# Layer norm, gated attention and an expert mixture on one core: another order of the fold, the first step and the last tiles, and another way for the bias column

## The chip, the cores and the metric

The kernel runs on one core of one Trainium2 chip. The metric is the device time of the kernel in microseconds (us). The engines are named as the profile names them: PE is TensorE's matrix multiply (PEld its weight load), DVE is VectorE, ACT is ScalarE, POOL is GpSimd, and SP is SyncE, which here only issues DMAs.

## The reference

The input x has 4 sequences of 1024 tokens with 512 features. Cut to what matters:

```python
xn = layernorm(x)
# attention on xn, with a layer norm of its own (gamma, beta)
x_norm = layernorm(xn) * gamma + beta
q, k, v = x_norm @ qkv[:, :512], x_norm @ qkv[:, 512:1024], x_norm @ qkv[:, 1024:]
attn = softmax(causal(q @ k.T / sqrt(512)))
s = (attn @ v) @ o_proj + xn
# experts on xn: 8 experts, the best 2 of each token, and a shared one
gates = top2_normalised(softmax(xn @ router_w.T))
routed = sum_e gates[:, e] * (silu(xn @ wg[e]) * (xn @ wu[e])) @ wd[e]     # inner width 352
shared = (silu(xn @ sg) * (xn @ su)) @ sd                                  # inner width 704
out = xn_input + s * silu(routed + shared)        # xn_input is x
```

## The kernel before

Matrices are multiplied in float16 pairs: each float32 operand is split into a high part (ACT writes it, `..._hi`, `high`) and a low part (DVE writes it, `..._lo`, `low`), and a product is three products of parts. PE's program is one long row of such products, in five stages.

**Fold** (`fold_programs`). The attention weights are multiplied together once: q with k, and v with o_proj. PE turns q and k by 128x128 transposes (eight groups, `("turn", m, n)`, each in a PSUM bank of its own), ACT and DVE split each bank. v is split, and SP turns it by four DMA transposes (L401) into `v_turned`. Then come eight products, `("product", m, n)` with m = 0 for q with k and m = 1 for v with o; `bank_of` names the bank of each. Beta gives a bias: DVE multiplies the bank of each turned q with a row of beta and sums it (`beta_row`, L602, four of them, after which the bank is free), PE multiplies small things (`beta_products`, `bias_folds`), and DVE writes `bias_q` and `bias_v` (`keep_bias`). `rows_before` says how many `beta_row` a product waits for. The load of beta and the load of o_proj count on one semaphore, `rest_loaded`. Between all this DVE also takes the statistics of the first two token tiles (`stats`, `normalise`), and splits the weights of the shared expert (`split_hi` on ACT and `split_lo` on DVE, eight pieces; pieces 0 to 3 are for gate and up, 4 to 7 for down).

**Shared expert** (`expert_stages`, the loops over `range(NT)`, 32 steps of one token tile, two units each). Unit n of PE is `unit_in` (24 matmuls, L677), and after it `unit_down` of unit n - 2 (9 matmuls, L684). A unit's chain is: PE, `silu` on ACT, `hidden` on DVE, `h_high` on ACT, `h_low` on DVE, `turn_h` on SP (a DMA transpose, L1079), and the landed transpose lets `unit_down` go. Beside it a step normalises a later tile, splits expert weights (`in_high`/`in_low` in chunks, `down_high`/`down_low`) and turns the tile (`turn_x`). All queues are served in program order, so a step that waits holds what stands behind it. Steps from `ROUTING` = 24 on also hold the routing tables, which DVE writes (`one_hot`) and PE multiplies (`hot_product`, L1283). At the end of step `LATE` + 1 = 27, ACT issues `store_bias` (L427): `bias_v`, 128 partitions of 4 floats, goes to the DRAM row `bias_row`, so that 512 single floats are written 512 bytes apart within a partition.

**Routed experts** (71 slot tiles in a hardware loop), then **attention** (`stage4`): for each sequence 16 projection groups, and 8 tiles of queries, in order `ORDER`, for the last sequence `LAST_ORDER` = 1, 3, 5, 0, 7, 4, 2, 6. A query tile t is: `scores` on PE (L1806), `soften` on DVE (mask, row maximum, L1942 to L1946), `probs` and `p_high` on ACT, `p_low` on DVE, two DMA transposes, `weigh` on PE (L1819, three matmuls for each block of 128 keys, bank `pv_banks[t % 2]`), `combine_first` and `combine` on DVE (L1967, L1975, L1979), `finish` on POOL (adds x, L1744), and the store. `end` on DVE makes the gate. PE weighs two tiles behind the scores, and `weigh(t)` waits for `combine(t - 2)`, which frees the bank.

## Time and profile before

| | us |
|---|---|
| median of three runs | 1174.65 |
| lowest, highest | 1174.34, 1176.52 |
| profiled execution, own time | 1174.52 |
| its span in the trace | 1172.8 |
| PE busy | 1140.6 |

The span runs from the first instruction of the trace to the last; 1.7 us of the profiled execution's own time lie outside it. Start times below are us from the start of the span. "Idle before" is how long the engine stood still, and the releaser is what ended that.

### The profile page before, as it was taken

How to read it: one execution, taken by the hardware profiler on the slowest of the kernel's cores; microseconds unless marked ns; L12 is line 12 of the kernel's file. 1: busy time of each engine (PE TensorE's matmuls, PEld its weight loads, DVE VectorE, ACT ScalarE, POOL GpSimd, SP SyncE). 2: the span in 40 equal slices, each digit the busy share in tenths (PEclk: the TensorE clock that was granted, in tenths of full speed). 3: DMA queues.
4: the chain of work that ended last, by engine and by line, in shares of the span. 5: the costliest groups of instructions: out<-in, count | busy, mean ns of one | idle time of the engine just before them, and what ended most of it. 6: DMA issues, size and time to landing. Idle time of an engine off the chain costs nothing. (4 is left out here: it accounts for less than half of the span.)

```text
span 1172.8 us, 21142 instructions
## 1 busy us (share of the span) xinstructions
PE 1140.6 (97%) x6608; PEld 628.7 (54%) x6609; DVE 568.8 (49%) x1168; ACT 470.2 (40%) x824; POOL 423.4 (36%) x659
## 2 busy tenths in 40 slices
PE   7999999999998999999999999999999999999996
PEld 4555555555555555555555555554444444444442
DVE  5876766676557422211211221221377467467466
ACT  4543444344422222322322322333655545645652
POOL 2253333332100122222222222211764764754754
PEclk9999999999999999999999999999999999999999
DMA  8879999989545588999899778776667767676373
GB/s 247 235 190 238 228 243 214 226 204 234 154 84 70 106 160 201 203 206 191 207 209 193 172 179 185 178 172 173 138 162 194 151 161 183 169 166 178 106 161 102
DMA packets 369410, 210.22 MB, mean 179 GB/s; under 512 B 308912, under 2 KB 319160, under 8 KB 369344
## 3 DMA queue, kind: packets, MB, share of 16 engines
q1 hardware_dynamic: 357984, 173.67, 64.5%
q0 software_dynamic: 10800, 35.69, 12.0%
q8 instruction: 36, 0.59, 0.2%
q14 instruction: 30, 0.25, 0.1%
q10 hardware_dynamic: 560, 0.02, 0.0%
HBM read 89.31 MB, written 46.01 MB: 115 GB/s over the span
## 5 line engine op out<-in xcount | busy, mean ns | idle before, releaser
L677 PE MATMUL pair<-arena 128*128 (+2 forms) x3240 | 506.4, 313 | 2.5 <-DVE arena L1466 1.5
L677 PEld LDWEIGHTS pair<-arena 128*128 128x128 f16 x3240 | 316.2, 98 | 185.6 <-issue 4.5
L684 PE MATMUL bank<-arena 128*128 (+1 forms) x1215 | 285.3, 380 | 9.6 <-DMA arena<-arena 9.6
L684 PEld LDWEIGHTS bank<-arena 128*128 128x128 f16 x1215 | 118.4, 98 | 137.9 <-DMA arena<-arena 8.2
L1531 DVE SCALAR_TENSOR_TENSOR arena<-pair,slot_unit,arena 128x352 f32<-128x352 f32 x71 | 41.4, 583 | 270.7 <-ACT arena L1447 229.5
L1447 ACT ACTIVATE arena<-pair,slot_unit 128x352 f32<-128x352 f32 x71 | 39.3, 553 | 207.1 <-PE pair L677 176.8
L1207 POOL COPY arena<-token_of 128x1 uint32 (+1 forms) x71 | 13.2, 186 | 278.8 <-DMA arena<-arena 98.4
L1819 PE MATMUL bank<-arena 128*128 128x512 f16 x432 | 98.3, 379 | 1.8 <-DVE arena L1975 1.8
L1806 PE MATMUL pair<-arena 128*128 128x512 f16 (+3 forms) x576 | 97.5, 326 | 0.6 <-ACT arena L1863 0.6
L1209 POOL DMA_INDIRECT arena<-xn_rows,arena x71 | 70.8, 998 | 55.6 <-POOL arena L1207 55.6
L1791 PE MATMUL bank<-arena 128*128 128x512 f16 x384 | 86.0, 379 | 1.6 <-PEq L1026 1.6
L1791 PE MATMUL pair<-arena 128*128 128x512 f16 x384 | 84.7, 379 | 0.0
L1806 PEld LDWEIGHTS pair<-arena 128*128 128x128 f16 x576 | 52.9, 98 | 45.8 <-ACT arena L1863 1.1
L1726 POOL DMA_INDIRECT arena<-slot_rows,arena x64 | 68.5, 1070 | 24.5 <-POOL arena L1723 21.5
L1364 ACT ACTIVATE arena<-pair,unit 128x352 f32<-128x352 f32 x64 | 35.1, 549 | 96.3 <-PE pair L677 96.0
L235 POOL TENSOR_TENSOR root_seed<-variances,minus_half 128x2 f32<-128x2 f32 x32 | 24.6, 770 | 129.8 <-DVE variances L245 129.8
L1819 PEld LDWEIGHTS bank<-arena 128*128 128x128 f16 x432 | 41.8, 98 | 50.5 <-issue 2.7
L1733 POOL TENSOR_TENSOR arena<-arena 128x512 f32<-128x512 f32 x32 | 42.4, 1325 | 65.2 <-ACT arena L1878 64.2
L1791 PEld LDWEIGHTS bank<-arena 128*128 128x128 f16 x384 | 37.5, 98 | 46.3 <-issue 2.0
L1791 PEld LDWEIGHTS pair<-arena 128*128 128x128 f16 x384 | 37.6, 98 | 45.3
L1744 POOL TENSOR_TENSOR arena<-arena 128x512 f32<-128x512 f32 x32 | 43.3, 1359 | 48.6 <-DVE arena L1979 48.4
L1466 DVE SCALAR_TENSOR_TENSOR arena<-pair,unit,arena 128x352 f32<-128x352 f32 x64 | 36.9, 577 | 47.6 <-ACT arena L1364 47.6
(186 smaller groups left out, 1178.5 us busy)
## 6 DMA issues: line engine op xcount, KB each, us to landing
slot_rows<-arena SPq DMA_DIRECT2D x71, 256.0 KB
arena<-in_L_attn_x_dram SPq DMA_DIRECT2D x64, 256.0 KB, 3.5
xn_rows<-arena SPq DMA_DIRECT2D x32, 260.0 KB, 2.6
shared_rows<-arena SPq DMA_DIRECT2D x32, 256.0 KB
arena<-shared_rows SPq DMA_DIRECT2D x32, 256.0 KB
out_dram<-arena SPq DMA_DIRECT2D x32, 256.0 KB, 2.2
arena<-in_L_ffn_wg_dram SPq DMA_DIRECT2D x32, 176.0 KB, 3.0
arena<-in_L_ffn_wu_dram SPq DMA_DIRECT2D x32, 176.0 KB, 3.3
```

What stands on the lines that cost most here:

```text
L677: last = pe.matmul(bank[:, 0:width], xt[:, a, c, :], weights(c, b, col, width), start=(c == 0 and i == 0), stop=(c == KC - 1 and i == 2))
L684: last = pe.matmul(bank[:, :], ht[:, a, c, :], weights(c, b), start=(start and c == 0 and i == 0), stop=(stop and c == HC - 1 and i == 2))
L1209: pool.indirect_dma_start(xg[u].bitcast(U32), None, xn_rows.bitcast(U32), bass.IndirectOffsetOnAxis(ap=index[u], axis=0)).then_inc(gathere ...
L1447: nc.scalar.activation(sbuf[u], g_banks[u][:, 0:H], ACT.Silu, scale=slot_unit[u][:, 0:1]).then_inc(slot_silu_done, 1)
L1466: v.scalar_tensor_tensor(sbuf[b], u_banks[b][:, 0:H], unit[:, t, 1:2], sbuf[b], ALU.mult, ALU.mult).then_inc(h_ready, 1)
L1531: v.scalar_tensor_tensor(sbuf[u], u_banks[u][:, 0:H], slot_unit[u][:, 1:2], sbuf[u], ALU.mult, ALU.mult).then_inc(slot_h_ready, 1)
L1726: pool.indirect_dma_start(c[f"y{n}", u], None, slot_rows, bass.IndirectOffsetOnAxis(ap=c[f"i{n}", u], axis=0)).then_inc(y_loaded[n][u], 16)
L1733: pool.tensor_tensor(c["y0", u], c["y0", u], c["y1", u], ALU.add).then_inc(y_summed, 1)
L1744: pool.tensor_tensor(c["res", u], c["s", t % S_AHEAD], c["x", t % X_AHEAD], ALU.add).then_inc(res_ready, 1)
L1791: last = pe.matmul(bank[:, :], left, right, start=(k == 0 and n == 0), stop=(k == KC - 1 and n == 2))
L1806: last = pe.matmul(wide[t % 2][:, col:col + w], qt[:, a, k, i * P:(i + 1) * P], x2t[b % 2][col // HALF][:, r, k, 0:w], start=(k == 0 and m ...
L1819: last = pe.matmul(pv_banks[t % 2][:, :], c["pt", t % 3][:, a * (i + 1) + k, :], vs[:, k, r, :], start=(k == 0 and n == 0), stop=(k == i a ...
```

## The change

1. **Fold.** Beta and o_proj get a semaphore each. The products (0,1) and (0,2) go to banks 6 and 7, (0,3) to bank 0, (1,0) to bank 1, and wait for none, none, one and two `beta_row`; the last three wait for the low parts of the first three instead. `beta_products` runs before the products of v and o. ACT and DVE run the same splits in another order.
2. **First step of the shared expert.** ACT and DVE get a written-out order, `first_step`: `h_high` and `h_low` of unit 0 stand ahead of the first chunk of expert weights, the down pieces 4 and 5 behind unit 1's `silu` and `hidden`, and `down_high`/`down_low` at the end.
3. **Bias.** PE turns `bias_v` (128x4) into 4x128 behind the first `unit_down` (`turn_bias`), ACT copies it at step 2 (`keep_bias_row`), and SP stores four rows of 512 bytes at step 4 (`store_bias`). The store on ACT at step 27 is gone.
4. **Last tiles.** DVE's `soften` of the last tile stands ahead of `combine` of the fourth tile before it; `end` of the last tile stands behind.
5. **Last product.** `weigh_last` computes columns 0 to 255 first (`pv_banks[1]`), then 256 to 511 (`proj_banks[0]`), 21 matmuls each of 256 columns in place of 21 of 512; `combine_last` does both halves on DVE, the addition of x with it, and SP stores each half. POOL's `finish` of the last tile is gone.

```diff
-            bank_of = list(range(2 * KC)) + [4, 0, 1, 2, 6, 7, 4, 3]
-            rows_before = (0, 1, 2, 3, 0, 0, 0, 4)
+            bank_of = list(range(2 * KC)) + [4, 6, 7, 0, 1, 4, 6, 7]
+            rows_before = (0, 0, 0, 1, 2, 0, 0, 0)
...
-                sp.dma_start(beta_rows, beta.partition_broadcast(P)).then_inc(rest_loaded, 16)
-                sp.dma_start(w_o, o_proj.rearrange("(c p) n -> p c n", p=P)).then_inc(rest_loaded, 16)
+                sp.dma_start(beta_rows, beta.partition_broadcast(P)).then_inc(beta_loaded, 16)
+                sp.dma_start(w_o, o_proj.rearrange("(c p) n -> p c n", p=P)).then_inc(o_loaded, 16)
...
-            def store_bias(act):
-                act.wait_ge(bias_made, 2)
-                act.dma_start(bias_row.rearrange("(c p) -> p c", p=P), bias_v[:, :],
-                              allow_slow_non_contiguous=True).then_inc(bias_stored, 16)
+            def store_bias(sp):
+                bias_row_kept(sp)
+                sp.dma_start(bias_row.rearrange("(c p) -> c p", p=P), affine_rows[0:KC, :]).then_inc(bias_stored, 16)
...
+            def turn_bias(pe):
+
+                pe.wait_ge(bias_made, 2)
+                pe.transpose(small[0:KC, 0:P], bias_v[:, :], ident).then_inc(group_done, 1)
+
+            def keep_bias_row(act):
+
+                act.wait_ge(group_done, len(on_pe) + 1)
+                nc.scalar.copy(affine_rows[0:KC, :], small[0:KC, 0:P]).then_inc(hi_done, 1)
...
+                    def first_step():
+
+                        silu(0, 0)
+                        h_high(0, 0)
+                        for i in in_chunks(0):
+                            in_high(i)
+                        silu(1, 1)
+                        split_hi(act, IN_SPLITS)
+                        split_hi(act, IN_SPLITS + 1)
+                        for t in normal_in(0):
+                            x_high(t)
+                        h_high(1, 1)
...
+                    def first_step():
+
+                        for t in normal_in(0):
+                            stats(dve, t)
+                        hidden(0, 0)
+                        keep_logits(0)
+                        h_low(0, 0)
+                        for i in in_chunks(0):
+                            in_low(i)
+                        for t in normal_in(0):
+                            normalise(dve, t)
+                        hidden(1, 1)
+                        split_lo(dve, IN_SPLITS)
+                        split_lo(dve, IN_SPLITS + 1)
+                        h_low(1, 1)
...
+                        for cols, bank in zip(halves, last_banks):
+                            for k in range(i + 1):
+                                for n, (a, r) in enumerate(PARTS):
+                                    last = pe.matmul(bank[:, cols], c["pt", t % 3][:, a * (i + 1) + k, :],
+                                                     vs[:, k, r, cols], start=(k == 0 and n == 0), stop=(k == i and n == 2))
+                            last.then_inc(pv_done, 1)
...
+                        for n, cols in enumerate(halves):
+                            dve.wait_ge(pv_done, t + n + 1)
+                            v.scalar_tensor_tensor(row[:, cols], last_banks[n][:, cols], c["inv", u][:, 0:1], row[:, cols],
+                                                   ALU.mult, ALU.add).then_inc(s_made, 1)
+                            dve.wait_ge(s_made, t + n + 1)
+                            v.scalar_tensor_tensor(row[:, cols], row[:, cols], 0.5 / S_Q, g[:, t % QT, cols], ALU.mult, ALU.mult
+                                                   ).then_inc(o_made, 1)
+                            dve.wait_ge(o_made, t + n + 1)
+                            v.tensor_tensor(res[:, cols], row[:, cols], x_row[:, cols], ALU.add).then_inc(last_added, 1)
...
+                            if t == NT - 1:
+                                combine(t - 4)
                             if n > 2:
                                 combine_first(t - 3)
                             if n > 0:
                                 p_low(t)
-                            if n > 2:
+                            if n > 2 and t != NT - 2:
                                 combine(t - 3)
```

The order on DVE in the fold, before. L595 is `low` (bank 4 to 7: turned k; `arena<-arena`: v or o), L602 a `beta_row`, L241 begins `stats`, L253 to L261 are `normalise`:

```order
5 L595 SCALAR_TENSOR_TENSOR arena<-bank6,arena 128x512
6 L595 SCALAR_TENSOR_TENSOR arena<-bank7,arena 128x512
7 L602 ISA arena<-pair0,arena 128x512
...
9 L241 BN_STATS moments<-arena 128x6
...
13 L602 ISA arena<-pair0,arena 128x512
...
15 L595 SCALAR_TENSOR_TENSOR arena<-arena 128x512 x4
```

The same place now, where `low` is L611 and `beta_row` L618:

```order
L611 SCALAR_TENSOR_TENSOR arena<-pair,arena 128x512 x4
L241 BN_STATS moments<-arena 128x6
...
L611 SCALAR_TENSOR_TENSOR arena<-bank,arena 128x512 x4
L611 SCALAR_TENSOR_TENSOR arena<-arena 128x512 x4
...
L261 TENSOR_SCALAR arena<-arena,mean_var,kept 128x512
L611 SCALAR_TENSOR_TENSOR arena<-bank,arena 128x512
...
L618 ISA arena<-pair,arena 128x512
```

The four low parts of v, behind which SP turns v, moved ahead of every `beta_row`, and the statistics of tile 0 moved between the two halves of the turns.

ACT in the first step of the shared expert, before. L1364 is `silu`, L1376 `in_high`, L1370 `h_high`, L221 `split_hi`, L265 the high part of a token tile:

```order
23 L1364 ACTIVATE arena<-pair,unit 128x352
24 L1376 ACTIVATE arena<-arena 128x704
25 L1370 CAST arena<-arena 128x352
26 L221 ACTIVATE arena<-arena 128x2x512
27 L221 ACTIVATE arena<-arena 96x512
28 L265 CAST arena<-arena 128x512
29 L1380 ACTIVATE arena<-arena 128x512
30 L1364 ACTIVATE arena<-pair,unit 128x352
```

The same place now, where `silu` is L1389, `h_high` L1395 and `in_high` L1401:

```order
26 L1389 ACTIVATE arena<-pair,unit 128x352
27 L1395 CAST arena<-arena 128x352
28 L1401 ACTIVATE arena<-arena 128x704
29 L1389 ACTIVATE arena<-pair,unit 128x352
30 L221 ACTIVATE arena<-arena 128x2x512
31 L221 ACTIVATE arena<-arena 96x512
32 L265 CAST arena<-arena 128x512
33 L1395 CAST arena<-arena 128x352
```

Unit 0's `h_high` moved ahead of the chunk of expert weights, and unit 1's `silu` ahead of the down pieces and of tile 2.

DVE at the last tiles, before. L1951 is `p_low`, L1942 begins `soften`, L1975 and L1979 are `combine`, L1965 and L1967 `combine_first`:

```order
930 L1951 TENSOR_TENSOR arena<-arena 128x384
931 L1975 SCALAR_TENSOR_TENSOR arena<-bank,arena 128x512
932 L1979 SCALAR_TENSOR_TENSOR arena<-arena 128x512
933 L1942 TENSOR_TENSOR pair<-pair,arena 128x128
...
938 L1951 TENSOR_TENSOR arena<-arena 128x896
```

The same place now, where these lines are L2022, L2013, L2046 and L2050, L2036 and L2038:

```order
934 L2022 TENSOR_TENSOR arena<-arena 128x384
935 L2013 TENSOR_TENSOR pair<-pair,arena 128x128
...
938 L2046 SCALAR_TENSOR_TENSOR arena<-bank,arena 128x512
939 L2050 SCALAR_TENSOR_TENSOR arena<-arena 128x512
...
942 L2022 TENSOR_TENSOR arena<-arena 128x896
```

The last tile's `soften` moved ahead of one `combine`.

## Rows read from the trace of the kernel before

**Rows 1.** The page: each engine's busy time, share of the span and instructions

```profile
PE 1140.6 (97%) x6608; PEld 628.7 (54%) x6609; DVE 568.8 (49%) x1168; ACT 470.2 (40%) x824; POOL 423.4 (36%) x659
```

**Rows 2.** PE's waits: releaser, then us in total, times, longest

```profile
PE bank L684 <- DMA arena<-arena: 9.6, 8, 3.0
```

**Rows 3.** PE's timeline, fold and first steps: start, duration, line, count [idle before]

```profile
17.49 8.03 PE L486 MATMUL pair<-arena 128*128 128x512 f16 x36 [1.44 <-DVE arena L602]
26.37 2.76 PE L486 MATMUL bank<-arena 128*128 128x512 f16 x12 [0.85 <-DMA arena<-arena]
...
39.14 10.98 PE L677 MATMUL pair<-arena 128*128 128x360 f16 x72
51.30 2.10 PE L684 MATMUL bank<-arena 128*128 128x512 f16 x9 [1.17 <-DMA arena<-arena]
54.87 3.74 PE L677 MATMUL pair<-arena 128*128 128x352 f16 x24 [1.47 <-DVE arena L1466]
59.59 2.10 PE L684 MATMUL bank<-arena 128*128 128x512 f16 x9 [0.97 <-DMA arena<-arena]
```

**Rows 4.** DVE's timeline of the same stretch

```profile
12.14 2.48 DVE L595 SCALAR_TENSOR_TENSOR arena<-bank,arena 128x512 f16<-128x512 f32 x4 [1.65 <-ACT arena L553]
16.74 0.69 DVE L602 CUSTOM_DVE_ANT_0 arena<-pair,arena 128x512 f32<-128x512 f32 x1 [2.12 <-DMA arena<-in_L_attn_o_proj_dram]
...
19.18 2.49 DVE L595 SCALAR_TENSOR_TENSOR arena<-arena 128x512 f16<-128x512 f32 x4
...
33.03 1.61 DVE L226 SCALAR_TENSOR_TENSOR arena<-arena 128x1408 f16<-128x1408 f32 x1
...
47.88 0.52 DVE L1471 TENSOR_TENSOR arena<-arena 128x352 f16<-128x352 f32 x1
```

**Rows 5.** ACT's timeline: the first chunk of expert weights

```profile
46.25 0.79 ACT L1376 ACTIVATE arena<-arena 128x704 f16<-128x704 f32 x1 [2.73 <-DMA arena<-in_L_ffn_wu_dram]
```

**Rows 6.** The `turn_h` issued at 356.2, alone, and the time to its landing

```profile
L1079 SPq DMA_TRANSPOSE arena<-arena x1: 1211/1211/1211, 356.2 to 356.2; - x1
...
DMA to landing us min/median/max: 12.9/12.9/12.9
```

**Rows 7.** The store of the bias on ACT, and the time to its landing

```profile
L427 ACTq DMA_DIRECT2D bias_row<-bias_v x1: 417/417/417, 355.8 to 355.8; - x1
...
DMA to landing us min/median/max: 10.0/10.0/10.0
```

**Rows 8.** PE's timeline behind it

```profile
369.16 3.24 PE L684 MATMUL bank<-arena 128*128 128x512 f16 x9 [2.99 <-DMA arena<-arena]
372.20 0.69 PE L1283 MATMUL bank<-arena 128*128 128x71 f16 x8
372.69 4.09 PE L677 MATMUL pair<-arena 128*128 128x352 f16 x24
```

**Rows 9.** A stretch: length, busy us of engines, granted clock (PEclk), DMA share, GB/s

```profile
371.00:373.00 2.00, 2.00 (x14) 1.03 (x13) 2.00 (x6) 0.56 (x1) 0.00 (x0) 0.50 0.01 2
```

**Rows 10.** PE's timeline near the end

```profile
1111.80 1.47 PE L1806 MATMUL pair<-arena 128*128 128x256 f16 x12
...
1147.03 10.67 PE L1819 MATMUL bank<-arena 128*128 128x512 f16 x48
1159.52 4.69 PE L1819 MATMUL bank<-arena 128*128 128x512 f16 x21 [1.82 <-DVE arena L1975]
```

**Rows 11.** DVE's timeline at the end

```profile
1149.96 0.29 DVE L1942 TENSOR_TENSOR pair<-pair,arena 128x128 f32<-128x128 f32 x1
...
1156.84 1.68 DVE L1967 TENSOR_TENSOR arena<-arena 128x512 f32<-128x512 f32 x1
...
1164.36 0.75 DVE L1975 SCALAR_TENSOR_TENSOR arena<-bank,arena 128x512 f32<-128x512 f32 x1 [1.18 <-PE bank L1819]
1165.21 0.69 DVE L1979 SCALAR_TENSOR_TENSOR arena<-arena 128x512 f32<-128x512 f32 x1
```

**Rows 12.** POOL's timeline at the end

```profile
1165.98 1.26 POOL L1744 TENSOR_TENSOR arena<-arena 128x512 f32<-128x512 f32 x1 [1.69 <-DVE arena L1979]
```

160 lines of the change are left out of this document (97 added, 63 removed).

## The prediction

> **What bounds the kernel now.** I read the page first: PE is busy 1140.6 of 1172.8 us [rows 1], and no other engine passes half the span. So the kernel is as long as PE's program plus PE's stops, and a change that leaves the products alone can only win back stops, or the tail behind PE's last matmul. The waits of PE come next: the largest sum is unit_down waiting for its DMA transpose, 9.6 us in 8 waits [rows 2]. PE's timeline then says where the stops are. They lie in three places. In the fold and the first steps: 1.44, 0.85, 1.17, 1.47 and 0.97 us [rows 3]. At 369 us one of 2.99 us, behind which 9 matmuls take 3.24 us where they otherwise take 2.10 [rows 8, 3]. At the end 1.82 us ahead of the last product [rows 10], and then the tail: PE's last matmul ends at 1159.52 + 4.69 = 1164.2, POOL's addition at 1165.98 + 1.26 = 1167.2 [rows 10, 12], and the store takes what is left of the span, 5.6 us. Between these places PE hardly stops, so what is won in one of them should reach the end. I add the gains up against the profiled execution's own 1174.52 us, which is within 0.02% of the median, 1174.65.
>
> **Part 1, the fold.** The 1.44 us stop goes. PE's second product had to wait for a beta_row, and DVE began that at 16.74, when o_proj had landed [rows 4]. Now the second and third product need no beta_row, and run from 17.49 - 1.44 = 16.05 us on. Three products took 8.03 us [rows 3], 2.68 each, so the fourth starts at 21.4 and needs one beta_row. DVE's turns of k end at 12.14 + 2.48 = 14.6, the low parts of v take 2.49 more and end at 17.1 [rows 4], then come one normalise, one low part, three small operations and the beta_row, an estimate of 3.3 us: 20.4. That is 1.0 us early. The 0.85 us stop goes as well: SP turned v behind low parts that began at 19.18 [rows 4] and now begin at 14.6, so the first halves land near 26.37 - 4.6 = 21.8, and the first product of v and o comes at 16.05 + 3 x 2.68 + 0.8 for beta_products = 24.9. What is late next is the split of o_proj, which now stands behind three more operations on DVE; by the same counting it ends near 25.1, and its last quarter is needed at 26.8. So the fold ends 2.3 us earlier, and unit 0 starts at 39.14 - 2.29 = 36.85.
>
> **Part 2, the first step.** A unit takes 3.7 us (three in 10.98 [rows 3]). Units 0, 1 and 2 then end at 40.6, 44.4 and 48.1. DVE is nearly full in the fold: from 25.1 on it has four split pieces of 1.61 us [rows 4] and some 10.5 us of other work, and ACT keeps it waiting some 1.5 us, so hidden of unit 0 comes at 43.6. With h_high straight behind it, h_low ends at 45.1, not at 47.88 + 0.52 = 48.4 [rows 4]. The transpose took 51.30 - 48.4 = 2.9 us [rows 3], so it lands at 48.0, when PE arrives. But unit_down also wants down pieces 4 and 5, and here I expect the new stop. Their low parts stand on DVE behind the first chunk's low part, normalise of tile 2 and hidden of unit 1, and the chunk waits for its load, which landed at 46.25 [rows 5]. I let it land 1.9 us earlier, as the normalise of tile 1 ahead of it on SP does. Then 44.4 + 5.5 us of work (0.8 on ACT, 0.9, 1.4, 0.6 and 1.8 on DVE) is 49.9, and unit_down starts at 50.0 against 51.30. Behind it the 1.47 us stop is gone (hidden of unit 1 is long done), unit 3 ends at 55.7, and the next transpose, behind tile 2's on SP, lands near 56.2 against 59.59. So PE is 3.4 us ahead there. The one added transpose on PE costs at most a small matmul's 0.2 us, and sits on the path: **3.2 us** for parts 1 and 2. The ends: 0.8 us if DVE falls another 2.4 us behind, 4.9 us if all five stops of rows 3 go, less one small one. The few later stops of 0.8 to 1.3 us up to 110 us I leave as they are, since the chains of the tiles move as PE does.
>
> **Part 3, the bias.** The turn_h issued at 356.2 took 12.9 us to land [rows 6], against 2.9 us at the start. In between lies the bias store, issued 0.4 us before it and landed after 10.0 us [rows 7]: at 365.8, and the transpose at 369.1, just where PE goes on. It moves 2 KB, but as 512 single floats. Without that hold the transpose lands at 359.1, seven us before PE needs it. The stop of 2.99 us goes, and so does what the slow clock cost behind it: 3.24 - 2.10 = 1.14, some 0.25 of the 0.69, and 4.09 - 3.74 = 0.35 [rows 8, 3]. The granted clock falls from 1.00 to 0.50 there, 2.4 to 1.2 GHz, after PE had stood 3 us [rows 9]. The sum is 4.7 us. DVE writes one_hot tables there almost without a pause, and only won part of that time, so PE meets it sooner at the hot products; I give back 0.5: **4.2 us**, ends 3.0 and 4.7. In its place PE gets the one transpose (counted), ACT one copy of 4x128 at step 2, with slack on ACT, and SP one store of four rows at step 4, 0.4 us of issue on a queue that waits for its tiles there anyway.
>
> Here a rule speaks against me. What the rows show is one transpose of 12.9 us beside one store of 10.0 [rows 6, 7]. The Trainium skill ("DMA: Bandwidth & Descriptors", section "Queues, rings and completion order") says that each DMA engine takes turns between the queues a packet at a time, so another queue's transfer should delay a transpose by its turns, not by its whole length. By the rule the hold has another cause and stays, and the sum has 0 here in place of 4.2.
>
> **Part 4, the last tiles.** The last soften began at 1149.96, behind a combine of 1.4 us [rows 11]; now it is first, and its softmax and transposes come 1.4 us earlier. The 1.82 us stop before the last product was for combine of the tile two before it [rows 10], which in turn stood behind end and a combine_first held to 1.68 us by POOL [rows 11]. PE is through with that tile's product after 39 of the 48 matmuls, at 1147.03 + 39 x 0.222 = 1155.7 [rows 10], and DVE can now take it at once: done at 1156.6, before PE wants to go on at 1157.7. So that stop goes too.
>
> **Part 5, the last product.** 12 matmuls of 256 columns took 1.47 us [rows 10], 0.11 each when the tail of the last is taken off, so 42 take 4.7 us, as 21 of 512 did. PE ends near 1162.5, not 1164.2. But then DVE is late. It has end, combine_first and combine of the tile before, and combine_first of the last: with two holds by POOL's finishes of up to 1.1 us each, combine of the tile before ends near 1161.5, and its next addition at 1162.2. Then six half operations of 0.4 to 0.5 us (0.75 and 0.69 for whole ones [rows 11]), the second of which waits for POOL until about 1163.4: the last ends near 1165.4, against 1167.2 for POOL before [rows 12]. The 5.6 us behind stay. **1.9 us** for parts 4 and 5; 3.3 us if POOL never holds DVE, and 0.8 if the last transposes are late or each hold is doubled.
>
> **The sum.** 3.2 + 4.2 + 1.9 = 9.3 us, and 1174.5 - 9.3 = **1165.2 us**.
>
> **The rivals.** (A) The hold at 356 us is not the store's, or ends elsewhere: parts 1, 2, 4 and 5 alone, 5.1 us, **1169.4**. Against it speaks that the store and the transpose begin and end within 0.4 and 3.3 us of each other. (B) The fold gives nothing: DVE is the full engine there, each beta_row and split only changed places, and PE stops at unit 1 or at the first unit_down for pieces that come as late as before. Then 4.2 + 1.9 = 6.1 us, **1168.4**. For it speaks that my DVE schedule has margins of about 1 us over some 25 operations. (C) Both: 1.9 us, **1172.6**. (D) The slower one: the store of the bias holds the transposes whatever its form, and has only moved from step 27 to step 4. There the transposes have no spare time (7 us at 359): a hold of 12.9 - 2.9 = 10 us falls on PE whole, with 1.7 us of slow clock behind. Then 3.2 + 4.2 + 1.9 - 11.7 = -2.4, **1176.9**. It decides from a hold of some 7.6 us on. Against it: four rows of 512 bytes are 4 pieces, not 512. (E) It does not do what it says: the last product in halves ends no earlier, since DVE has twice the operations. That is inside the low end of part 5.
>
> **How the numbers follow.** The forecast of 1165.2 with its bounds has 0.64, (A) 0.12, (B) 0.13, (C) 0.05, (D) 0.05, and 0.01 is for the rest. The bounds of the parts give gains from 0.8 + 3.0 + 0.8 = 4.6 to 4.9 + 4.7 + 3.3 = 12.9 us, 1161.6 to 1169.9. Both ends at once are unlikely at the fast side, so the range is 1162.0 to 1170.5, which takes in (A) and (B) and leaves out (C) and (D). A measurement of this kernel can tell about 0.2%, 2.3 us, from no change: faster 0.89 (forecast, A, B), same 0.06 (C and the rest), slower 0.05 (D).
>
> **What would show it.** Part 1: no stop ahead of the second product, and unit 0 starting at 36.9. Part 2: h_low of unit 0 before 45.5, a first unit_down near 50 released by DVE's split, not by the DMA. Part 3: no stop near 360, all turn_h landing in 3 to 5 us there, the clock 1.00 throughout, and the store of four rows landing in some 2 or 3 us with no longer stops around step 4. Parts 4 and 5: the last product following the one before without a pause, and DVE's last addition near 1158.0 in its own trace (1165.4 less the 7.4 us won before). The prediction is wrong if a transpose behind the new store takes over 8 us, or if PE stops for over 3 us in the first step, where the clock would fall as well.

## The result, and the profile after

The changed kernel takes 1162.55 us (median of four runs, 1161.58 to 1162.77), against 1175.59 for the kernel before in the same session. The ratio is 0.9885, with a 95% interval of 0.9866 to 0.9904: faster by 1.15%, 13.0 us. The forecast was 1165.2 with a range of 1162.0 to 1170.5. The profiled span went from 1172.8 to 1160.6 us, 12.2 us less. That is what the rows below have to explain.

The page (compare [rows 1]): TensorE's busy time is the same to 0.2 us, so in sum the gain is stops and tail.

```profile
span 1160.6 us, 21195 instructions
PE 1140.8 (98%) x6630; PEld 630.9 (54%) x6631; DVE 564.5 (49%) x1172; ACT 471.0 (41%) x825; POOL 425.4 (37%) x658
```

PE's waits (compare [rows 2]: 9.6 us in 8 waits on the same transposes):

```profile
PE bank L702 <- DMA arena<-arena: 4.7, 2, 3.4
PE bank L1890 <- DMA arena<-arena: 1.2, 1, 1.2
```

PE's timeline of fold and first steps (compare [rows 3]; L695 is `unit_in`, L702 `unit_down`, L541 the turned bias). The last row is a later place without a stop before it, which had 113.73 before:

```profile
16.42 5.35 PE L486 MATMUL bank<-arena 128*128 128x512 f16 x24
...
36.97 10.98 PE L695 MATMUL pair<-arena 128*128 128x360 f16 x72
47.82 2.10 PE L702 MATMUL bank<-arena 128*128 128x512 f16 x9
49.76 0.27 PE L541 MATMUL bank<-arena,bias_v 128*4 128x128 f32 x1
49.87 3.74 PE L695 MATMUL pair<-arena 128*128 128x352 f16 x24
57.01 4.00 PE L702 MATMUL bank<-arena 128*128 128x512 f16 x9 [3.40 <-DMA arena<-arena]
...
110.08 2.11 PE L702 MATMUL bank<-arena 128*128 128x512 f16 x9
```

The way to read such a pair of traces is the **lead**: the start of one and the same piece of work before, less its start after. It is 39.14 - 36.97 = 2.17 us at unit 0, 3.48 at the first `unit_down` (51.30 against 47.82), 5.00 at unit 3 (54.87 against 49.87), and only 2.58 at the next `unit_down` (59.59 against 57.01), since there stands a stop of 3.40 us that nobody had before. Behind it 9 matmuls take 4.00 us in place of 2.10, and a stretch of the table by windows has the granted clock at 0.50, that is 1.2 in place of 2.4 GHz:

```profile
58.00:60.00 2.00, 2.00 (x7) 0.63 (x5) 1.59 (x3) 1.88 (x4) 1.94 (x2) 0.50 1.11 268
```

At 65 us the lead is gone. At 110 us it is back, 3.65 us (113.73 against 110.08): the stops of 1.3, 0.9 and 0.8 us that the kernel before still has up to there are missing now. At 344 us it is still 3.65. These are the leads of one pair of executions; how far they differ in others is told ahead of the experiments. Then comes the place of the bias store. The `turn_h` transposes from 340 to 400 us land in 2.7 to 4.5 us (compare [rows 6]) and PE has no stop for them (compare [rows 8]):

```profile
L1098 SPq DMA_TRANSPOSE arena<-arena x10: 1211/1216/1581, 341.5 to 394.9; - x10
...
DMA to landing us min/median/max: 2.7/2.7/4.5
```

Behind it the lead is 8.07, so the bias gave 4.42 us. Between 400 and 1110 us it grows to 8.85. Most of that is the slot tiles of the routed experts: there PE stands for DMA transposes of such tiles for 1.01 us in two places before and for 0.31 in one now. The rest, 12.2 - 8.85 = 3.35 us, is won at the end. PE's, DVE's and POOL's timelines there (compare [rows 10 to 12]):

```profile
1138.18 10.52 PE L1878 MATMUL bank<-arena 128*128 128x512 f16 x48
1149.90 4.76 PE L1890 MATMUL bank<-arena 128*128 128x256 f16 x42 [1.20 <-DMA arena<-arena]
```

```profile
1155.73 0.48 DVE L2063 SCALAR_TENSOR_TENSOR arena<-bank,arena 128x256 f32<-128x256 f32 x1 [1.80 <-DMA out_dram<-arena]
...
1158.02 0.43 DVE L2069 TENSOR_TENSOR arena<-arena 128x256 f32<-128x256 f32 x1
```

```profile
1153.35 1.71 POOL L1803 TENSOR_TENSOR arena<-arena 128x512 f32<-128x512 f32 x1 [2.28 <-DVE arena L2050]
```

The last addition ended at 1167.24 before (POOL) and ends at 1158.45 now (DVE): a lead of 8.79, no more than at 1138 us. By the last addition, then, parts 4 and 5 gave nothing. But behind it the span went on for 5.56 us before and goes on for 2.15 us now. What stands there is seen only in the instructions that end the block: on each queue a DRAIN, and behind it the semaphore by which the engines meet. Before, and after (count, duration in ns, start):

```profile
L1644 POOLq DRAIN  x1: 6611/6611/6611, 1165.9 to 1165.9; - x1
L1644 SPq DRAIN  x1: 7/7/7, 1169.5 to 1169.5; - x1
L1644 ACTq EVENT_SEMAPHORE  x1: 17/17/17, 1172.7 to 1172.7; - x1
```

```profile
L1700 POOLq DRAIN  x1: 7057/7057/7057, 1153.3 to 1153.3; - x1
L1700 SPq DRAIN  x1: 7/7/7, 1160.4 to 1160.4; - x1
L1700 ACTq EVENT_SEMAPHORE  x1: 17/17/17, 1160.6 to 1160.6; - x1
```

SP comes to its DRAIN once the stores have landed. Before that was at 1169.5, and everybody then waited 3 us more for POOL, whose DRAIN ended at 1172.5, 5.3 us behind the end of POOL's last addition. After, POOL's last addition (tile 30's) ends at 1155.06 and its DRAIN at 1160.4, again 5.3 us later, in the same tenth as the landing of the last store.

### The profile page after: what moved, and what is told of

The parts are those of the page before. It is cut to its first block and busy times, and to the rows that moved or that the text cites. A ratio compares the mean times of both kernels' runs of the same rounds, so it can differ in the third digit from the quotient of the medians.

```text
span 1160.6 us, 21195 instructions
## 1 busy us (share of the span) xinstructions
PE 1140.8 (98%) x6630; PEld 630.9 (54%) x6631; DVE 564.5 (49%) x1172; ACT 471.0 (41%) x825; POOL 425.4 (37%) x658
## 5 line engine op out<-in xcount | busy, mean ns | idle before, releaser
L695 PE MATMUL pair<-arena 128*128 (+2 forms) x3240 | 507.1, 313 | 0.3 <-DMA arena<-arena 0.3
L695 PEld LDWEIGHTS pair<-arena 128*128 128x128 f16 x3240 | 316.6, 98 | 183.7 <-issue 1.8
L702 PE MATMUL bank<-arena 128*128 (+1 forms) x1215 | 286.0, 381 | 4.7 <-DMA arena<-arena 4.7
L702 PEld LDWEIGHTS bank<-arena 128*128 128x128 f16 x1215 | 119.1, 98 | 132.1 <-issue 7.7
L1878 PE MATMUL bank<-arena 128*128 128x512 f16 x411 | 93.4, 379 | 0.0
L1850 PE MATMUL bank<-arena 128*128 128x512 f16 x384 | 86.0, 379 | 1.6 <-PEq L1045 1.6
L1389 ACT ACTIVATE arena<-pair,unit 128x352 f32<-128x352 f32 x64 | 35.3, 552 | 111.4 <-PE pair L695 110.6
```

The lines of the kernel that those rows point to most:

```text
L695: last = pe.matmul(bank[:, 0:width], xt[:, a, c, :], weights(c, b, col, width), start=(c == 0 and i == 0), stop=(c == KC - 1 and i == 2))
L702: last = pe.matmul(bank[:, :], ht[:, a, c, :], weights(c, b), start=(start and c == 0 and i == 0), stop=(stop and c == HC - 1 and i == 2))
L1850: last = pe.matmul(bank[:, :], left, right, start=(k == 0 and n == 0), stop=(k == KC - 1 and n == 2))
L1878: last = pe.matmul(pv_banks[t % 2][:, :], c["pt", t % 3][:, a * (i + 1) + k, :], vs[:, k, r, :], start=(k == 0 and n == 0), stop=(k == i a ...
```

## The experiments

Times below are of profiled spans unless they are called medians. Most of the kernels were run once, and one and the same code does not stand at the same time in every execution. The kernels of five of the runs below are the changed kernel up to 110 us (one of them but for the place of one small store). These are PE's times in them:

| trace | first product of the fold | unit 0 | the place at 110 us | from unit 0 to there |
|---|---|---|---|---|
| before | 12.89 | 39.14 | 113.73 | 74.59 |
| changed | 11.65 | 36.97 | 110.08 | 73.11 |
| four rows on ACT | 13.00 | 36.65 | 108.22 | 71.57 |
| last addition on POOL | 13.77 | 37.41 | 108.95 | 71.54 |
| in place | 12.13 | 35.77 | 110.23 | 74.46 |
| POOL done early | 14.43 | 38.07 | 110.97 | 72.90 |
| part 4 undone | 12.85 | 36.49 | 109.91 | 73.42 |

The first column differs with the loads of the first 10 us, the last one mostly with the slow clock. So the lead at 110 us, 3.65 us in the pair above, is anything from 2.8 to 5.5 us, and a difference of spans under some 3 us shows nothing by itself. I compare distances within a run where I can.

### The bias store

**Part 3 alone**, put into the kernel before (with PE's turn and ACT's copy of it):

```diff
-            def store_bias(act):
...
+            def store_bias(sp):
+                bias_row_kept(sp)
+                sp.dma_start(bias_row.rearrange("(c p) -> c p", p=P), affine_rows[0:KC, :]).then_inc(bias_stored, 16)
...
```

> The kernel before with part 3 of the change alone: the bias column is turned by PE, copied by ACT at step 2, and stored as four rows by SP at step 4. If the 512 single floats of the store made the hold of the transposes at 356 us, all turn_h there land in under 5 us, the stop of 2.99 us and the slow clock behind it go, and the span is 4.4 us shorter than 1172.8, near 1168.4 (4.42 us is what PE's program won there in the changed kernel). If the hold comes from something else at that place, the span stays within 1 us of 1172.8. If a store of the bias holds transposes whatever its form, a stop of some 10 us comes near 97 us and the span is over 1178.

Median 1170.52 (six runs) against 1174.77, ratio 0.9967 [0.9952, 0.9982]; the span is 1168.1, 4.7 us less. The `turn_h` of 340 to 400 us land in 2.7 to 4.3 us, PE has no stop for them, and the one of 1.82 us at the end stays as it was. Across the old place of the store the lead goes from -0.40 us (362.54 against 362.14) to 4.04 (387.05 against 391.09). So part 3 is worth 4.44 us by itself, as in the sum (4.42).

**Form, queue or place?** The change altered all three. So, in the changed kernel: the four rows, but on ACT at step 27, where the single floats had been (this store reads memory that is used for other things by then, so the bias in it is not the reference's).

```diff
-                        if s == 4:
-                            store_bias(sp)
...
+                        if s == LATE + 1:
+                            store_bias(act)
```

> The changed kernel with the store of the four rows back on ACT at the end of step 27, so that the queue and the place are those of before and only the form is new. If the form made the hold: no stop near 352 us, span within 0.7 us of the changed kernel's 1160.6. If the queue or the place made it: a turn_h of over 10 us and a stop of some 3 us there, span near 1165.

The `turn_h` there land in 2.7 to 3.9 us. The span is 1158.8, 1.8 us under the changed kernel's where at most 0.7 was expected; that lead, 1.86 us, is all there at 110 us already, most of it because the clock did not fall at 57 us in this execution. At the old place PE stops only for DVE's tables:

```profile
356.63 0.45 PE L1304 MATMUL bank<-arena 128*128 128x71 f16 x8 [0.55 <-DVE arena L955]
```

And the reverse, the 512 single floats on SP at step 4:

```diff
-                sp.dma_start(bias_row.rearrange("(c p) -> c p", p=P), affine_rows[0:KC, :]).then_inc(bias_stored, 16)
+                sp.dma_start(bias_row.rearrange("(c p) -> p c", p=P), bias_v[:, :],
+                             allow_slow_non_contiguous=True).then_inc(bias_stored, 16)
```

> The changed kernel, but the store at step 4 on SP takes the 512 single floats from bias_v, as the store before did; queue and place are the new ones. If the form holds the transposes wherever it stands, the next transposes on SP take some 10 us longer, PE stops for 7 to 10 us near 97 us with a slow clock behind it, and the span is 8 to 12 us over 1160.6. If the hold needs a second queue (the store on ACT's, the transposes on SP's), the span stays within 1 us.

The span is 1170.0, 9.4 us more, and 8.9 of them are there at the first table products (367.38 against 358.49). The transpose of a token tile issued behind the store took 12.1 us to land (first fence), the hidden pieces' one 12.4, and PE stood 6.09 us for it (second fence):

```profile
L284 SPq DMA_TRANSPOSE arena<-arena x1: 1244/1244/1244, 95.9 to 95.9; - x1
...
DMA to landing us min/median/max: 12.1/12.1/12.1
```

```profile
110.84 4.02 PE L703 MATMUL bank<-arena 128*128 128x512 f16 x9 [6.09 <-DMA arena<-arena]
```

The hold belongs to the form. With single floats it is there from ACT at step 27 and from SP at step 4 (12.9, 12.1, 12.4 us). With four rows it is in neither place: behind the changed kernel's store at 93.3 the transposes up to 125 us land in 2.7 to 4.0 us. That settles rivals A and D. Nor does it hold transposes alone: in this last run the plain store of a token tile issued at 97.2 took 11.9 us and the load of x at 97.8 took 11.5, where the load at 89.7, ahead of the floats, took 3.4.

### The first step

**Part 2 undone**, the new order of the fold kept:

```diff
-                        if s == 0:
-                            first_step()
-                            continue
...
+                        if s == 0:
+                            split_hi(act, IN_SPLITS)
+                            split_hi(act, IN_SPLITS + 1)
```

> The changed kernel with part 2 undone: ACT and DVE do the first step of the shared expert in the order of before, the fold as changed. If the fold's order alone brings what parts 1 and 2 bring together (3.65 us at 110 us), unit_down of unit 115 stands where it did in the changed kernel. By my sum the fold gives 2.2 us at unit 0 and the first step's order the rest: then stops of 1 to 1.5 us come back ahead of the first unit_down and of unit 3, and PE is at 110 us some 2 us ahead of the kernel before, span near 1162.

The span is 1164.3. The gain of the fold is there at first (`unit_down` at 48.68 against 51.30) and is then handed back in the old order's own stops:

```profile
52.27 3.74 PE L695 MATMUL pair<-arena 128*128 128x352 f16 x24 [1.38 <-DVE arena L1491]
56.88 2.10 PE L702 MATMUL bank<-arena 128*128 128x512 f16 x9 [0.88 <-DMA arena<-arena]
81.05 2.12 PE L702 MATMUL bank<-arena 128*128 128x512 f16 x9 [1.57 <-DMA arena<-arena]
100.80 3.73 PE L702 MATMUL bank<-arena 128*128 128x512 f16 x9 [2.62 <-DMA arena<-arena]
```

The `unit_down` that has 110.08 after and 113.73 before is at 113.58 here: a lead of 0.15. About 2 us had been expected. So in this execution the fold's lead of 2.27 us at unit 0 (36.87) is handed back by 110 us; 1.63 us of that is the slow clock behind the stop of 2.62 us (3.73 us for 9 matmuls), which another execution need not have. From unit 0 to the 110 us place it takes 76.71 us, against 71.5 to 74.5 in the six traces with the written-out first step: that is worth 2.2 to 5.2 us. What it moved is the chain of token tiles. POOL's memset behind the low piece of tile 3 starts at 64.65 before, at 62.05 here and at 58.24 after; counted from the start of unit 0 that is 25.5, 25.2 and 21.3 us.

**The 3.40 us stop.** SP's timeline around it in the changed kernel (L284 turns tile 2, L290 stores it, L1050 is a load, L1098 is `turn_h(1)`):

```profile
50.54 1.24 SPq L284 DMA_TRANSPOSE arena<-arena  x1
51.82 0.58 SPq L290 DMA_DIRECT2D xn_rows<-arena  x1
52.45 0.44 SPq L1050 DMA_DIRECT2D arena<-in_L_attn_x_dram  x1
52.93 1.22 SPq L1098 DMA_TRANSPOSE arena<-arena  x1
```

DVE had the hidden pieces ready at 47.64 + 0.51 = 48.15, but SP stood before the tile until 50.54. I put `turn_h(1)` ahead of the tile:

```diff
+                        if s == 1:
+                            turn_h(1)
                         for t in routed_in(s)[:1]:
                             pass_x(t)
...
-                        if s > 0:
+                        if s > 1:
                             turn_h(2 * s - 1)
```

> The changed kernel, but at step 1 SP issues the transpose of unit 1's h ahead of the transpose, store and load of tile 2. h_low of unit 1 is ready at 48.2 and its transpose is issued at 52.9 in the changed kernel, behind tile 2's. My theory: that order on SP makes the stop of 3.40 us at 57; here it lands by 52 and the stop is gone, with the slow clock. But PE then runs into what the chain of the token tiles allows: that chain is 6.4 us earlier than in the kernel before (the last x_low ahead of POOL's memset ends at 58.2 against 64.6), PE at 110 us only 3.65, so some 2.7 us are to be had, the rest comes back as stops between 60 and 115 us. Span near 1158. Rival: nothing limits it behind, and the whole 3.4 us and the clock's 3 us are won: 1154. Other rival: the transpose of tile 2 comes later and PE stops for it instead: 1160.

The stop is gone, and the clock stays there. But the span is 1162.3. Other stops of the same kind came in its place, and behind the longest the clock fell after all (granted clock 0.50 from 101 to 103 us):

```profile
61.78 2.12 PE L702 MATMUL bank<-arena 128*128 128x512 f16 x9 [0.26 <-DMA arena<-arena]
79.44 2.12 PE L702 MATMUL bank<-arena 128*128 128x512 f16 x9 [0.88 <-DMA arena<-arena]
98.86 3.22 PE L702 MATMUL bank<-arena 128*128 128x512 f16 x9 [2.30 <-DMA arena<-arena]
```

At the 110 us place PE is at 111.63. This run had begun late, with unit 0 at 39.31; from there it took 72.32 us, which is inside the 71.5 to 74.5 of the same code without the edit. So no gain can be told from this run, and the later span is no loss either.

**The chain of the tiles.** One long link of it is a memset of 6.92 us on POOL, in front of tile 4's seed. I moved it to step 12, alone and then with the edit above:

```diff
                     x_low(pool, 3)
-                    if HR < P:
-                        pool.wait_ge(shared_lo, len(splits))
-                        pool.memset(w_down[HR:P, :, HC - 1], 0.0).then_inc(down_padded, 1)
-                        pool.wait_ge(down_padded, 1)
...
                     for s in range(2, LATE):
+                        if HR < P and s == 12:
+                            pool.wait_ge(shared_lo, len(splits))
+                            pool.memset(w_down[HR:P, :, HC - 1], 0.0).then_inc(down_padded, 1)
+                            pool.wait_ge(down_padded, 1)
```

> The changed kernel with one edit: GpSimd's memset of the down weights' padding rows (6.92 us at 58.24 in the changed kernel's trace, between the low piece of tile 3 and the seed of tile 4) goes from there to step 12 of the unit loop. If the stops that came back when the hidden pieces' transpose was put ahead (0.26, 0.88 and 2.30 us at 61.8, 79.4 and 98.9) are those of the chain of the next token tiles, this memset is one of its links: the seed of tile 4 comes up to 6.9 us earlier. Alone, with the 3.4 us stop still there (it belongs to a transpose queued behind another on the sync queue), TensorE should gain nothing: the unit_down after the stop at 57.0, the one at 110 us within 0.3 us of 110.08, span 1160.3 to 1160.9. Rival: the tiles' chain held in the changed kernel too, hidden in short stops: then 0.5 us or more less at 110 us. A second rival: the memset costs at step 12 what it cost at step 1, and a stop appears near 130 us: longer by up to 3 us.

Alone it gives nothing: PE is 1.29 us later than in the changed kernel right behind the long stop (58.30 against 57.01, the loads came later here), and 1.10 later at 110 us (111.18 against 110.08). From unit 0 that is 74.47 us, the slow end of the spread. The span is 1161.8.

> Both edits together: the transpose of the hidden pieces of unit 1 ahead of that of token tile 2 on the sync queue, and GpSimd's 6.92 us memset moved to step 12. With the first edit alone the stops behind 57 us came back as 0.26, 0.88 and 2.30 us, and unit_down stood at 111.63 at a place where the changed kernel has 110.08. If the memset is the link that makes them, they go, and so does the 3.4 us stop with the slow clock behind it (1.9 us): the unit_down at 110 us at 105.0 to 107.0 and the span 3 to 5 us below 1160.6, 1155.6 to 1157.6. Rival: the chain of the tiles has another pace (each tile's transpose waits for its turn among the hidden pieces' transposes on the same queue): the 0.9 and 2.3 us stops stay, and the span is 1160 to 1162.5.

Together they do: the 2.30 us stop shrank to 0.86 and 0.29, the clock did not fall there, and PE is at 106.97 at the 110 us place, as expected, and 3.1 us ahead at the table products (355.38 against 358.49). From unit 0 to the 110 us place it takes 68.75 us, 2.8 less than the shortest of the six. The span is 1159.0, not the 1155.6 to 1157.6 expected, for PE then stood for the transpose of a slot tile. It was issued at 599.4 and took 9.1 us to land, where those at 588.3 and 614.0 took 3.8 and 3.5; what held it no run shows:

```profile
608.68 3.75 PE L695 MATMUL pair<-arena 128*128 x24 [1.90 <-DMA arena<-arena]
```

### The last tiles

**Part 4 undone**, the last softmax back behind the combination:

```diff
-                            if t == NT - 1:
-                                combine(t - 4)
...
-                            if n > 2 and t != NT - 2:
+                            if n > 2:
                                 combine(t - 3)
```

> The changed kernel with its part 4 alone undone: the last query tile's softmax on VectorE goes back behind the combination of tile 28 and the end of the last group, and the last product's two halves stay. Forecast then: part 4 gave 1.0 to 1.1 us, so the stop ahead of the last product grows from 1.20 us (changed kernel) to about 2.3 us and the span from 1160.6 to 1161.6 or 1161.7. By what the changed kernel's trace shows (the lead did go from 8.85 to 9.62 at the last product, 0.8 us): about 0.8 us longer, 1161.4. Rival: the end is that of GpSimd's drain alone, 5.3 us behind its last addition, which a later softmax moves later only as far as GpSimd's last addition (tile 30) moves; with the combination of tile 28 done earlier this addition could even be earlier, and the span be 1160.6 or less in spite of the longer stop.

```profile
1138.15 10.68 PE L1878 MATMUL bank<-arena 128*128 128x512 f16 x48
1150.65 4.74 PE L1890 MATMUL bank<-arena 128*128 128x256 f16 x42 [1.82 <-DVE arena L2046]
```

The old stop of 1.82 us for `combine` is back, the last product is 0.75 us later, and the span 0.4 us longer (1161.0). The 48 matmuls ahead start within 0.03 us of each other in the two traces, so the difference is that of the tail. Part 4 gave 0.4 us, not 1.0. Why the last product gained no more than 0.75 stands in the two timelines of SP and DVE. With part 4 the last softmax begins 1.4 us earlier (1139.67 against 1141.09), but its two transposes are issued 0.65 us later (1145.52 against 1144.87): on SP they stand behind the store of the tile that DVE now combines later and POOL finishes later, at 1144.58. Part 4 removed the wait for `combine` and put one for the transposes, 1.20 us, in its place. And the span did not even get those 0.75 us, for it ends behind POOL and not behind PE: POOL's last addition ends at 1155.43 here and at 1155.06 with part 4, 0.37 us apart, and the span ends 5.57 and 5.54 us behind that.

**What sets the end?** First, the last halves' addition of x on POOL and not on DVE:

```diff
-                            v.tensor_tensor(res[:, cols], row[:, cols], x_row[:, cols], ALU.add).then_inc(last_added, 1)
...
+                        pool.wait_ge(o_made, t + n + 1)
+                        pool.tensor_tensor(c["res", u][:, cols], c["s", t % S_AHEAD][:, cols], c["x", t % X_AHEAD][:, cols],
+                                           ALU.add).then_inc(last_added, 1)
```

> The changed kernel, but POOL adds x to the two halves of the last tile, in place of DVE. In both traces so far the span ends 5.3 us after POOL's last addition ends (its drain of 6.6 and 7.1 us), and not with the last store. If POOL's drain sets the end, then with POOL's last addition near 1158.9 the span ends near 1164.2, 3.6 us over 1160.6. If the last store sets it, the end moves by what POOL's half additions take longer than DVE's, under 1 us.

POOL's last addition ends at 1156.26, its DRAIN at 1161.6, and the span is 1161.8, though the stores had landed at 1158.2. The end is 8.3 us behind PE's, against 5.9 in the changed kernel.

```profile
L1700 POOLq DRAIN  x1: 6071/6071/6071, 1155.5 to 1155.5; - x1
L1700 SPq DRAIN  x1: 7/7/7, 1158.2 to 1158.2; - x1
```

Second, the wait that the change put on DVE. DVE's `combine_last` writes into the buffer of tile 29, so it waits for that tile's store, issued at 1151.1; DVE stood 1.80 us for it. Written in place instead, it has no such wait:

```diff
-                        dve.wait_ge(res_stored[u], t // 2 * 16)
...
-                            v.tensor_tensor(res[:, cols], row[:, cols], x_row[:, cols], ALU.add).then_inc(last_added, 1)
+                            v.tensor_tensor(row[:, cols], row[:, cols], x_row[:, cols], ALU.add).then_inc(last_added, 1)
...
-                        sp.dma_start(OUT_FLAT[r:r + P, cols], c["res", u][:, cols]).then_inc(res_stored[u], 16)
+                        sp.dma_start(OUT_FLAT[r:r + P, cols], c["s", (NT - 1) % S_AHEAD][:, cols]).then_inc(res_stored[u], 16)
```

> The changed kernel, but the last tile's result is written over its own row and stored from there, so that DVE does not wait for the store of the tile two before (1.80 us of wait in the changed kernel's trace). DVE's last addition then ends some 1.8 us earlier against PE's end (1158.45 - 1154.66 = 3.8 us behind it in the changed kernel, 2.0 us here). If POOL's drain behind its last addition sets the end, the span still ends 5.9 us behind PE's end, as in the changed kernel. If the last store sets it, it ends some 4.1 us behind.

DVE's last addition ends 2.5 us behind PE, not 3.8, and the stores have landed at 1159.4. The span is 1160.9 all the same, for POOL's DRAIN ends at 1160.7:

```profile
L1700 POOLq DRAIN  x1: 7056/7056/7056, 1153.6 to 1153.6; - x1
L1700 SPq DRAIN  x1: 7/7/7, 1159.4 to 1159.4; - x1
```

Third, both: in place, and DVE adds x for tile 30 too, so that POOL is done one tile earlier.

```diff
-                    for t in range(NT - 3, NT - 1):
-                        finish(t)
+                    finish(NT - 3)
...
                     combine(NT - 2)
+                    finish_here(NT - 2)
```

> As e5, and DVE also adds x for the tile before the last, so that POOL's last addition is that of the third tile from the end. If POOL's drain sets the end, it now lies 5.3 us behind an addition that ends 3.6 us before PE does, the last store takes over, and the span ends 4.0 to 4.5 us behind PE's end: 1.5 to 2 us less than in the changed kernel. If the drain is of no account, the added DVE work of 0.7 us makes it end no earlier than e5.

Median 1162.39 (1161.74 to 1164.27, four runs), ratio 0.9895 [0.9876, 0.9914]. Now POOL's DRAIN (from 1150.8) is over at 1157.8, the stores have landed at 1160.9, and the span is 1161.1: 5.05 us behind PE's end (1156.05) against 5.94. So 0.9 us came off the tail where 1.5 to 2 was expected. DVE's extra addition stands in front of the last halves, so its last addition is 2.87 us behind PE and not 2.5. The medians show no difference from the changed kernel.

That POOL's last work sets the end holds over all the traces: in twelve of fourteen the span ends 5.5 to 5.6 us behind the end of POOL's last addition, wherever DVE and the stores were. Only in the two where POOL stops a tile earlier (this one and the next) is it 8.6 and 8.7 us, and there the landing of the last store ends the span.

**All three edits** together (`turn_h(1)` ahead, memset at step 12, this end):

> Three edits of the runs before in one kernel: the hidden pieces' transpose of unit 1 ahead of tile 2's on the sync queue, GpSimd's 6.92 us memset at step 12, and the end in which GpSimd's last addition is that of tile 29 (VectorE adds the input for tile 30, and the last halves are written in place, so that no wait on the output's store is left). The two edits of the beginning gave 3.1 us at the first slot product (355.38 against 358.49 us in the changed kernel); the end alone had the span 5.05 us behind TensorE's end instead of 5.94. If they add, and no wait for a weights load of 1.9 us falls at 608 us as in the run with the two, the span is 1160.6 - 3.1 - 0.9 = 1156.6 us, the range 1155.8 to 1158.5, and the timed median 3.5 to 4.5 us below the changed kernel's 1162.55 (ratio to the kernel before 0.985 to 0.986). Rival: the gain of the beginning is taken back in the slots by loads that come at their own pace (the stop at 608 us grows as TensorE gets earlier): then it is 1158 to 1159.5 in the span, and the 1.9 us stop is there again.

Median 1157.95 (1157.09 to 1160.34, four runs) against 1173.68, ratio 0.9873 [0.9853, 0.9894]; the span is 1155.4. It is that of the fastest of the four, and just under the range expected; the ratio is above the 0.985 to 0.986 expected. From unit 0 to the 110 us place PE takes 69.43 us, 2.1 less than the shortest of the six. Its page has no stop over 1.7 us, and its end is 5.1 us behind PE's:

```profile
60.49 2.12 PE L702 MATMUL bank<-arena 128*128 128x512 f16 x9 [0.61 <-DMA arena<-arena]
100.28 2.12 PE L702 MATMUL bank<-arena 128*128 128x512 f16 x9 [0.23 <-DMA arena<-arena]
```

```profile
L1703 POOLq DRAIN  x1: 6996/6996/6996, 1145.1 to 1145.1; - x1
L1703 SPq DRAIN  x1: 7/7/7, 1155.1 to 1155.1; - x1
```

The median is 4.6 us below the changed kernel's of another session, and its ratio to the kernel before is lower by 0.0012 only, with intervals that overlap (the kernel before was itself faster in that session). The span says 5 us, the ratio 1.4 us: that it is faster than the changed kernel is likely, how much is open.

## Why the prediction was right, and where it was not

The measured 1162.55 us lies in the range, but only 0.55 us inside its fast end: the gain was larger than the sum by a third. The sum went by parts as follows, the measured ones from the one pair of traces:

| | forecast | measured |
|---|---|---|
| parts 1 and 2 | 3.2 | 3.65 (lead at 110 and 344 us; 2.8 to 5.5 in six traces) |
| part 3 | 4.2 | 4.42 |
| stops in the slot tiles | 0 | 0.78 |
| parts 4 and 5 | 1.9 | 3.35 |
| sum | 9.3 | 12.2 |

**Part 3** was right in mechanism and size. The bound from one pair of rows held, and the experiments took the rivals away. The rule that I set against it, in the Trainium skill, "DMA: Bandwidth & Descriptors", section "Queues, rings and completion order", that each DMA engine takes turns between queues a packet at a time, does not bear out here as I used it: a transpose on SP behind a 512-float store on ACT landed in 12.9 us, where 2.7 is usual. Why the turns do not protect the transpose was not tried.

**Part 1** was right: the 1.44 us stop is gone, and unit 0 starts at 36.97, forecast 36.85. That these two agree so well is luck. The first product began 1.24 us earlier than before, for the loads had come earlier, and took 4.43 us in place of 2.76 (granted clock 0.51 from 11.6 to 14 us); the two nearly cancel. The fair comparison is from the first product to unit 0: 26.25 us before, 23.96 by the forecast, and 23.64 or 23.65 in the eight traces of the new fold without the slow clock, a gain of 2.6 us. With part 2 undone it came to 0.15 us at 110 us. Rival B named the right weakness, and part 2 is what answered it.

**Part 2** came to the right sum by wrong steps. I had the first `unit_down` at 50.0, held by DVE's down pieces. It started at 47.82 without a stop. The hold itself was as forecast: the second of those pieces was done at 45.90 + 1.82 = 47.72, just as PE arrived, and in seven other traces with this first step PE stood 0.80 us there and went on 0.1 us behind them. With the four rows on ACT they were done at 46.83 + 1.81 = 48.64. The profile names no releaser, but this `unit_down` waits in the program for just these pieces:

```profile
48.74 2.10 PE L702 MATMUL bank<-arena 128*128 128x512 f16 x9 [0.80 <-issue]
```

The step that failed was the time of `hidden` of unit 0: DVE took it up at 41.50, not at 43.6, and everything behind was early by as much. I had the next `unit_down` at 56.2 behind a short stop. It came at 57.01 behind 3.40 us, and the text had named a stop of over 3 us there as what would make it wrong. Half of this I had in hand ("behind tile 2's on SP, lands near 56.2"), but unit 3 was forecast to end at 55.7 and ended at 53.6, so a wait of 0.5 became one of 3.4, and with it came the slow clock. What made up for both was the sentence "The few later stops of 0.8 to 1.3 us up to 110 us I leave as they are, since the chains of the tiles move as PE does". They do not: the chain of tiles was 6.4 us earlier (58.24 against 64.65) when PE had no lead left, and so those stops went. Two errors of 3 to 4 us each cancelled, and that the parts came within 0.45 us of their sum is luck too.

**Part 4** was mis-sized: the combine's stop went, as forecast, but 0.4 us was won where the sum had about 1. I looked at what DVE does ahead of the last softmax and not at what SP has to issue ahead of its transposes, nor at POOL, whose last addition came only 0.37 us earlier by it.

**Part 5** was right in PE's end (the halves took 4.76 us against 4.69, so they cost nothing), and in the place of DVE's last addition by accident: forecast 1158.0, measured 1158.45. The holds by POOL that I counted are one (1.68 us at 1149.93), and the wait for the output buffer, in plain sight in the diff as `dve.wait_ge(res_stored[u], t // 2 * 16)`, I did not price: 1.80 us. The step that failed most is "the store takes what is left of the span, 5.6 us" and "the 5.6 us behind stay". It was not the store. The stores had landed 3.0 us before POOL's DRAIN was over, so what the change really won at the end is that POOL's last work moved from 1167.24 to 1155.06, 12.18 us: all of the gain in the span. The chain that ended last had said so, in its last pieces, which I had not read:

```profile
1162.59 1.43 POOL arena L1744
1164.02 1.92 issue
1165.95 1.30 POOLq L1644
```

Against the last product's start, the span ends 13.3 us later before, 10.35 with part 4 undone and 10.7 in the changed kernel: 2.9 us for part 5 and, with its 0.75 us earlier product, 0.4 for part 4.

## What to carry to other kernels

When an early part gets faster, look at which chain feeds PE later, and by how much that chain moved, not at PE's own lead: here the lead was zero at 65 us and 3.65 at 110, and one stop removed by hand came back as three until a link of 6.9 us was taken out of the chain. Before a lead is put down to an edit, look at the same code in other executions: here it stood at one place anywhere from 108.2 to 111.0 us. When a step is put ahead of another, look on every queue for what that other one lets go. And before the time behind the last store is given to the store, read each queue's last instructions: here the engine that finished its own work late set the end, and moving one addition away from it was worth more than doing it faster.

## What the runs showed of the hardware

- POOL's DRAIN at the end of the block was over some 5.3 us after the end of POOL's last addition in all fourteen traces, whether that addition came early or late. DVE's DRAIN took 0.5 to 0.8 us in all and was over within 0.1 us of DVE's last operation. What POOL does in its own no row shows.
- 2 KB stored as 512 single floats made the transposes issued 0.4, 2.4 and 4.8 us behind it land 12.9, 12.1 and 12.4 us after their own issue, the first from the other queue and the others from the same; a plain store and a load behind it took 11.9 and 11.5 us. The same 2 KB as four rows held none.
- A stop of about 3.5 us was followed by the slow clock in some runs and not in others, and the 9 matmuls behind it took 4.00 us (3.40 and 3.71 us of stop), 3.63 (3.64) or 2.10 (3.48). Shorter ones had it too: 3.22 us behind a stop of 2.30, 3.73 behind one of 2.62. So such a stop costs up to 2 to 3 us more in some executions, and I would now give it a range rather than a price.
- VectorE's low piece of 896 columns took 2.12 us while GpSimd added (1143.41) and 1.09 us when it did not. The Trainium skill, "GPSIMD Engine Reference", section "Specifications", has GpSimd and VectorE share their interfaces to SBUF and contend where VectorE reads two inputs from there, and the trace agrees. It is not always VectorE that pays: at 1146.98 its addition of 512 columns took the usual 0.67 us, and GpSimd's, begun at 1147.07, took 1.72 in place of 1.26. In these pairs the one that began later was the longer.
